# A cross-product kernel: one part of its combined weights computed row by row on TensorE instead of being moved there by DMA, and a coarser alternation of two kinds of work

## The reference

```python
# x: [512, 39, 64]   W0: [39, 39, 128]   W1: [39, 128, 128], all float32
x0 = h = x
outs = []
for W in (W0, W1):
    h = einsum('bid,bjd,ijh->bhd', x0, h, W)
    outs.append(h)
return concatenate(outs, axis=1).sum(axis=-1)      # [512, 256]
```

## Time and profile before

| what | value |
|---|---|
| median of 3 runs | 436.07 us (432.43 to 438.65) |
| profiled execution | 436.33 us, span 434.5 us |
| PE busy | 269.7 us, 62% |
| DVE, ACT, POOL busy | 160.5, 84.1, 77.5 us |
| DMA moved | 27.65 MB |
| TensorE clock, mean of the span | 0.847 |

### The profile page before, as it was taken

One profiled execution on the slowest core, in us unless ns is written; L12 is line 12 of the kernel. 1 busy time (PEld: TensorE's weight loads), 2 busy tenths in 40 slices (PEclk: granted clock), 3 DMA queues, 4 the chain that ended last, 5 costly groups with the idle time before them and its releaser, 6 DMA issues.

```text
span 434.5 us, 16676 instructions
## 1 busy us (share of the span) xinstructions
PE 269.7 (62%) x7930; PEld 235.2 (54%) x7930; DVE 160.5 (37%) x266; ACT 84.1 (19%) x105; POOL 77.5 (18%) x69
## 2 busy tenths in 40 slices
PE   5999400000000000998879797996978969789897
PEld 2448400000000000997778696895977859688796
DVE  0200001000000000996269906829369194691600
ACT  2661000000000000011113133231332313323300
POOL 2000000000000000100009910804407025070000
PEclk9999955555555555799998999998999999999999
DMA  8623475444444438001113121221212212100010
GB/s 306 277 34 38 55 124 132 42 55 51 46 51 51 47 47 178 23 5 34 34 32 82 55 74 39 70 72 32 63 51 65 54 56 63 51 8 14 7 20 8
DMA packets 25044, 27.65 MB, mean 64 GB/s; under 512 B 5712, under 2 KB 19600, under 8 KB 24720
## 3 DMA queue, kind: packets, MB, share of 16 engines
q1 hardware_dynamic: 24976, 26.59, 29.2%
HBM read 18.40 MB, written 0.52 MB: 44 GB/s over the span
## 4 chain that ended last, share of the span: by engine, by line
PE 55%; SPq 28%; issue 9%; DVE 4%; DMA 3%; ACT 0%; POOL 0%; POOLq 0%
SPq L252 28%; PE psum L458 24%; PE psum L437 15%; PE psum L396 7%; PE psum L414 6%; DMA arena<-arena 3%; PE psum L466 2%; DVE arena L345 2%; PE psum L472 1%; DMA arena<-in_w 1%; DVE arena L318 1%; DVE arena L329 0%; DVE arena L327 0%; ACT arena L360 0%; SPq L256 0%
## 5 line engine op out<-in xcount | busy, mean ns | idle before, releaser
L414 PE MATMUL psum<-arena 128*32 128x128 f32 x1690 | 54.1, 283 | 126.4 <-DVE arena L345 125.8
L220 POOL COPY arena<-arena 128x72 f32<-128x72 f32 x32 | 68.5, 2141 | 313.0 <-DMA arena<-in_x 171.6
L377 ACT COPY arena<-psum 128x920 f32<-128x920 f32 x64 | 61.1, 984 | 314.1 <-PE psum L437 314.0
L414 PEld LDWEIGHTS psum<-arena 128*32 128x32 f32 x1690 | 50.7, 113 | 130.1 <-DVE arena L345 126.3
L458 PE MATMUL psum<-arena 128*64 128x128 f32 x1840 | 111.2, 277 | 0.6 <-issue 0.6
L458 PEld LDWEIGHTS psum<-arena 128*64 128x64 f32 x1840 | 103.7, 138 | 6.1 <-issue 5.9
L437 PE MATMUL psum<-arena 64*32 64x115 f32 x4096 | 65.0, 265 | 29.5 <-issue 26.7
L437 PEld LDWEIGHTS psum<-arena 64*32 64x32 f32 x4096 | 54.9, 106 | 37.8 <-issue 37.8
L345 DVE TENSOR_TENSOR arena<-arena,psum 128x512 f32<-128x512 f32 (+1 forms) x29 | 18.4, 680 | 113.0 <-DMA arena<-arena 97.1
L318 DVE TENSOR_TENSOR arena<-arena 128x1600 f32<-128x1600 f32 x32 | 58.0, 1812 | 0.0
L336 DVE TENSOR_TENSOR arena<-psum,arena 64x256 f32<-64x256 f32 x8 | 3.3, 417 | 88.5 <-ACT arena L368 88.5
(11 more groups left out here) (13 smaller groups left out, 38.1 us busy)
## 6 DMA issues: line engine op xcount, KB each, us to landing
arena<-in_x SPq DMA_DIRECT2D x32, 312.0 KB, 3.1
arena<-arena SPq DMA_DIRECT2D x40, 57.5 KB
arena<-in_w SPq DMA_DIRECT2D x2, 768.0 KB, 7.8
arena<-in_v_first SPq DMA_DIRECT2D x1, 1520.0 KB, 11.4
arena<-in_v_second SPq DMA_DIRECT2D x1, 1520.0 KB, 14.5
arena<-in_c_x SPq DMA_DIRECT2D x2, 704.0 KB, 11.2
arena<-arena SPq DMA_DIRECT2D x24, 50.0 KB
arena<-arena SPq DMA_DIRECT2D x24, 47.5 KB
```

Source lines behind the costliest of these rows:

```text
L220: nc.gpsimd.tensor_copy(view(to, TO, (1, COPY0)), view(x + X_MAIN + 21, T, (1, COPY0)))
L377: nc.scalar.copy(view(s0[n % 2] + 8 * in_batch, (1, 2), (B, SLOTS), (2, GROUP)), bank_view(at, (BANK, 2), (GROUP, SLOTS), (1, GROUP))).the ...
L414: done = nc.tensor.matmul(bank_view(bank * BANK + j % IN_BANK * HID, (1, HID), rows=(ROWS * c, ROWS * c + ROWS)), view(v0 + row * ROWS, (1 ...
```

## The change

It has three parts. **Own weights in row form:** for each of the 128 hidden columns k and each strip c, one matmul with 32 places of W1 (read with a step of 32 words) as the stationary side and the 115 pairs as the moving side; the result has places on rows. Eight k fill two PSUM banks, and ACT copies them at once into `c0` (16 copies of 128 x 920, written with a step of 128 words). The 128 DMAs and the clearing of `c0` are gone; three DVE multiplications by a 0/1 mask clear what must not stand there. W1 is laid out in four pieces of 32 hidden columns. The loads of x, `w0_t2` and `c1_x` follow the tables directly, and DVE makes the first four units of products ahead of the masks. **Ends of batches:** `stage(n-2)` goes to the start of batch n, `take_out(n-3)` in place of `take_out(n-2)` ahead of its second unit, `store(n-2)` to its third. **Alternation:** the sums of four groups (16 pairs), then half a batch of weighing.

```diff
-        SUMS_BEHIND = {16: 0, 20: 1, 24: 2, 28: 3}
-        PRODUCTS_BEHIND = {7: 0, 10: 1, 13: 2, 16: 3}
+        SUMS_BEHIND = {10: 0, 15: 1, 20: 2, 25: 3}
...
 # gpsimd
-            nc.gpsimd.memset(view(c0, (1, ZEROED * HID)), 0.0).then_inc(c_zeroed, 1)
-                if u < PROD_RING:
-                    pool.wait_ge(c_landed, C_LANDED)
-                    pool.wait_ge(out1_ready, 2)
-                else:
+                if u >= PROD_RING:
                     pool.wait_ge(filled, 2 * (u - PROD_RING + 1))
...
 # sync
-            sp.wait_ge(c_zeroed, 1)
-            for i, (g, which, q) in enumerate(DIRECT):
-                sp.wait_ge(direct_copied, i + 1)
...
-                for f in range(4):
-                    sp.dma_start(view(c0 + j * HID, (HID, SLOTS - j), (1, HID), rows=(row + f, row + f + 1)),
-                                 view(d0[c] + (4 * g - ROW0[which] + f) * HID, (1, HID), rows=(j, SLOTS)))\
-                        .then_inc(c_landed, 16)
...
+            sp.dma_start(view(mask0, (1, len(MASKED))), mask).then_inc(mask_loaded, 16)
+            for u in range(BATCH_UNITS):
+                load_x(u)
+            (w0_t2 and c1_x, four DMAs, then load_x(4), load_x(5))
...
-                if turn == 1 and n >= 2:
+                if turn == 2 and n >= 2:
                     store(n - 2)
...
 # vector
-            dve.wait_ge(c_landed, C_LANDED)
+            products(0); products(1); (adds of out1); products(2); products(3)
+            dve.wait_ge(direct_copied, DIRECT)
+            dve.wait_ge(mask_loaded, 16)
+            for i, (j0, j1) in enumerate(MASKED):          # 15, 5 and 5 slots of 128 words
+                c = view(c0 + j0 * HID, (1, words))
+                mult(c, c, view(mask0 + i, (0, words)), ALU.mult).then_inc(c_masked, 1)
+            dve.wait_ge(c_masked, len(MASKED))
             for k in range(MIXED):
...
-                if k in PRODUCTS_BEHIND:
-                    products(PRODUCTS_BEHIND[k])
...
-                if turn == 2 and n >= 2:
-                    take_out(n - 2)
+                if turn == 1 and n >= 3:
+                    take_out(n - 3)
...
 # scalar
-                nc.scalar.copy(view(d0[2 * q + which] + (4 * g - ROW0[which]) * HID, (1, 4 * HID), rows=(0, SLOTS)),
-                               bank_view(i % DIRECT_BANKS * BANK, (1, 4 * HID), rows=(0, SLOTS)))\
-                    .then_inc(direct_copied, 1)
+                nc.scalar.copy(view(c0 + 8 * i, (4, 2), (1, 4), (HID, SLOTS)),
+                               bank_view(i % 4 * 2 * BANK, (BANK, 2), (SLOTS, 4), (1, SLOTS))).then_inc(direct_copied, 1)
...
+                if in_batch == 0 and n >= 2:
+                    stage(n - 2)
                 act.wait_ge(filled, g + 1)
...
-                if in_batch == 2 and n >= 2:
-                    stage(n - 2)
...
 # tensor
+            for i in range(DIRECT):                        # 16
+                if i >= 4:
+                    pe.wait_ge(direct_copied, i - 3)
+                for k in range(8 * i, 8 * i + 8):
+                    piece, at = divmod(k, PIECE)           # PIECE = 32
+                    if at == 0:
+                        pe.wait_ge(w1_loaded[piece], 16)
+                    for c in range(4):
...
+                        done = nc.tensor.matmul(
+                            bank_view((i % 4 * 2 + k % 8 // 4) * BANK + k % 4 * SLOTS, (1, SLOTS),
+                                      rows=(ROWS * c, ROWS * c + ROWS)),
+                            view(w1_0 + piece * PLACES * PIECE + ROW0[c % 2] * PIECE + at, (PIECE, ROWS)),
+                            view(u0 + c % 2 * LIST + c // 2 * SLOTS, (1, SLOTS)), start=True, stop=True)
+                done.then_inc(direct_filled, 1)
...
-            for u in range(BATCH_UNITS, UNITS):
-                n, turn = divmod(u, BATCH_UNITS)
-                sums(2 * u)
-                sums(2 * u + 1)
-                weigh(n - 1, turn)
-            for turn in range(BATCH_UNITS):
+            for g in range(BATCH_GROUPS, GROUPS):
+                n, in_batch = divmod(g, BATCH_GROUPS)
+                sums(g)
+                if in_batch % TURN == TURN - 1:            # TURN = 4
+                    weigh(n - 1, in_batch // TURN)
+            for turn in range(TURNS):                      # TURNS = 2
                 weigh(BATCHES - 1, turn)
```

More of the change, by code:

```diff
@@ L71, with masked_rows @@
 V_ROWS = len(v_tables())
+MASKED = [(0, 15), (15, 20), (20, COPY0 + 16)]
+def masked_rows(which, q, j):
+    if which:
+        return q == 0 or j < COPY1 + 4
+    return q == 0 and j < 20
 def cin_kernel(nc: bass.Bass, x: bass.AP, u_list: bass.AP, w1: bass.AP, v_first: bass.AP, v_second: bass.AP,
-               w0_t2: bass.AP, c1_x: bass.AP, out: bass.AP):
+               w0_t2: bass.AP, c1_x: bass.AP, mask: bass.AP, out: bass.AP):
     P, ALL_PAIRS, _ = x.shape
-    HID = w1.shape[2]
+    HID = w1.shape[1]
     HALF = P // 2
@@ L168, in cin_kernel @@
         out_stored = sem("out_stored")
[L170 to L183, removed]
         FIRST_LIST, SECOND_LIST = lists()
@@ L228, in load_x, with load_w1 @@
                              x[:, u * UNIT:(u + 1) * UNIT, :]).then_inc(x_loaded[u % X_RING], 16)
-            def load_u(which):
+            def load_w1(i):
+                words = PLACES * PIECE
+                sp.dma_start(view(w1_0 + i * words, (1, words)), w1[i]).then_inc(w1_loaded[i], 16)
+            for which in range(2):
                 sp.dma_start(view(u_raw0 + 2 * which * LIST, (1, 2 * LIST)), u_list[which]).then_inc(u_loaded[which], 16)
[L233 to L241, removed]
+            for i in range(PIECES):
                 load_w1(i)
@@ L296, in _ @@
             mult = nc.vector.tensor_tensor
-            for which in (1, 0):
+            for which in range(2):
                 raw = u_raw0 + 2 * which * LIST
@@ L304, in _ @@
             add(v, v, view(v_second0, (1, V_ROWS * ROWS)), ALU.add).then_inc(v_ready, 1)
[L305 to L308, removed]
             def products(u):
@@ L338, in take_out @@
                     view(stage0, (1, 2 * HID), rows=(0, HALF)), ALU.add).then_inc(out_ready, 1)
-            dve.wait_ge(c_landed, C_LANDED)
+            products(0)
+            products(1)
+            dve.wait_ge(out1_loaded, 64)
+            for at, second, words in ((w0_t2_0, w0_t2_second0, 4 * HID), (c1_x0, c1_x_second0, CROSS * HID)):
+                w = view(at, (1, words))
+                add(w, w, view(second, (1, words)), ALU.add).then_inc(out1_ready, 1)
+            products(2)
+            products(3)
+            dve.wait_ge(direct_copied, DIRECT)
+            dve.wait_ge(mask_loaded, 16)
+            for i, (j0, j1) in enumerate(MASKED):
+                words = (j1 - j0) * HID
+                c = view(c0 + j0 * HID, (1, words))
+                mult(c, c, view(mask0 + i, (0, words)), ALU.mult).then_inc(c_masked, 1)
+            dve.wait_ge(c_masked, len(MASKED))
             for k in range(MIXED):
@@ L385, in _ @@
         def _(pe):
-            for i, (g, which, q) in enumerate(DIRECT):
-                for piece, (f0, _) in enumerate(W1_PIECES):
-                    if 4 * g == f0 and (i == 0 or DIRECT[i - 1][0] != g):
-                        pe.wait_ge(w1_loaded[piece], 16)
[L390 to L397, removed]
-                                 view(w1_0 + 4 * g * HID, (1, 4 * HID)), start=True, stop=True).then_inc(direct_filled, 1)
+            for i in range(DIRECT):
+                if i >= 4:
[3 more added lines that the diff above has]
+                    if at == 0:
+                        pe.wait_ge(w1_loaded[piece], 16)
+                    for c in range(4):
+                        if k == 0 and c < 2:
+                            pe.wait_ge(u_ready, c + 1)
+                        done = nc.tensor.matmul(
[4 more added lines that the diff above has]
+                done.then_inc(direct_filled, 1)
             def mixed(k):
@@ L557 @@
                 v[1, :, row, r] = w0[field(c), field(l)]
-    laid_out = (("x", places[:, :, X_PLACES]), ("u_list", u_list.reshape(2, hid, -1)), ("w1", w1_places),
+    mask = _np.ones((128, len(MASKED)), f32)
+    for c in range(4):
+        for i, (j, _) in enumerate(MASKED):
+            if masked_rows(c % 2, c // 2, j):
+                at = ROWS * c + (N0 if c % 2 else N1)[0] - ROW0[c % 2]
+                mask[ROWS * c:ROWS * c + ROWS, i] = 0
+                mask[at:at + 8, i] = 1
+    w1_pieces = w1_places.reshape(hid, PLACES, 4, -1).transpose(2, 0, 1, 3)
+    laid_out = (("x", places[:, :, X_PLACES]), ("u_list", u_list.reshape(2, hid, -1)), ("w1", w1_pieces.reshape(4, hid, -1)),
                 ("v_first", v[0].reshape(hid, -1)), ("v_second", v[1].reshape(hid, -1)),
-                ("w0_t2", w0_t2.reshape(2, 128, -1)), ("c1_x", c1_x.reshape(2, 128, -1)))
+                ("w0_t2", w0_t2.reshape(2, 128, -1)), ("c1_x", c1_x.reshape(2, 128, -1)), ("mask", mask))
```

53 lines of the change are left out of this document (25 added, 28 removed).

## The result

The changed kernel takes **314.9 us** (median of 4 runs, 312.32 to 317.25) against 435.78 for the one before in the same session: ratio 0.7208, 95% interval 0.7128 to 0.7289. Its profiled execution has a span of 313.7 us. The chip has a slower state in some executions: medians here are over all runs, ratios over the fast runs alone.

The account below looks back on a forecast made before the run. SP's 128 DMAs were taken to bound the kernel until 174.3 us, then PE's work with stalls. Unit 8 at 136.6, six batches of 22.9 to 274.0, last weighing 14.4 and end 3.2: span 291.6, plus 1.8 outside, 293; range 280 to 322.

Parts of the forecast that it names:

- rival A: Sums: double bursts outrun instruction loads, PE stops 1.85 us in each of about 13 bursts, +24, 317 us; chance 0.12.
- The 128 DMAs bounded the start: Start: SP's list of 128 DMAs is the bound until 174.3 us; 121 us of the gain come from there.
- Own weights at 29.7 us and 2.0 of slow start: Own weights: 512 matmuls take 28 to 31 us, taken as 29.7, plus 2.0 for PE's slow first stretch; end at 37.8.
- rival E: Start: instruction loads crawl beside 372 GB/s of tables, so PE is not the bound: +5 us, inside the range; no separate chance.
- The start at 6.1: PE's start moves from 5.1 to some 6.1 us, as some 0.25 MB more loads ahead at 372 GB/s.
- Masks under cover: DVE's masks take 3.5 us to 44.5, covered by 6 us before PE first needs an addition at 51.9.
- Mixed stage, DVE's late unit, POOL's wait: Mixed stage ends at 102.3; DVE makes unit 4 after the last addition, 0.6 + 4.15 us; PE waits 4.5 before unit 8.
- just level with the work, so I add 0.7 for stops: Each batch: six instruction blocks take 22.3 us at 3.7 against 22.2 of work; with 0.7, 22.9 a batch, six 137.4.
- Two turns less save 0.4 us: Alternation: a turn to weighing costs 0.2 us, so two turns less save 0.4 us of a batch.
- The ends of batches get loose: New orders give DVE its lead; it needs 16.6 + 0.4 us a batch, less than PE.
- Rival C: Ends of batches: DVE still waits once per batch for an ACT copy, about 4 us x 5: 313 us; chance 0.05.
- 22 from the stalls: Of the 143 us forecast gain, 121 come from the start and 22 from the stalls.

Follow-up runs that it names:

- a4: Changed kernel with the old ends of batches and sums of two groups, then a quarter of weighing, leaving only the first part: 309.9 us, ratio 0.716.
- a6: Changed kernel, but SP issues everything behind W1 (tables, mask, x) only when the own weights have been copied: 335.6 us.
- a3: Changed kernel with `stage`, `take_out` and `store` back at their old places, half batches of weighing kept: 309.4 us, ratio 0.715.
- a1: Changed kernel with sums of two groups, then a quarter of the weighing, in place of four groups and half: 307.2 us, ratio 0.708.
- b1: Kernel before with only `stage`, `take_out` and `store` moved to their new places: 422.9 us, ratio 0.979.
- c1: Changed kernel with products of units 4 to 7 made among the additions, and sums of two groups, then a quarter of weighing: 301.8 us, ratio 0.690.
- c2: The c1 kernel with SP waiting for the first piece of W1 before it issues anything behind it: 299.1 us, ratio 0.694.
- s1: Changed kernel with 40 PE waits without work put once ahead of unit 4's sums: 315.2 us.
- t8: Changed kernel with the sums of a whole batch, then the whole weighing of the one before: 326.5 us.

## Why the prediction was right, and where its sizes were off

The forecast was 293, the range 280 to 322, the time 314.9. That is inside the range, but outside the 280 to 308 that had a chance of 0.70, and close to rival A's 317. What carried the gain was foreseen; how much the stops would take was not. By its own terms, from the spans (291.6 forecast, 313.7 measured):

| term | forecast | measured |
|---|---|---|
| start of PE | 6.1 | 8.3 |
| own weights | 31.7 | 37.0 |
| mixed stage | 64.5 | 63.7 |
| last block to unit 8 | 34.3 | 34.3 |
| six batches | 137.4 | 152.7 |
| last weighing and end | 17.6 | 17.8 |

- **The 128 DMAs bounded the start:** right. The waits of 125.4 and 97.1 us are gone, and a4, with this part alone, has 309.9, so the first part carries all of the gain that is left. It also moved the loads of x and the products of the first four units; no run parts these from the row form.
- **Own weights at 29.7 us and 2.0 of slow start:** PE's pace was right (27.3 ns a record, 28 us in all), and the slow start cost its 2.0 (0.7 in a6). The term of the sum that was off is the stops: 5.6 us where the 29.7 had room for 1.7, since I took the block pace of 3.7 us for this stage too; and the lower clock behind the longest of them cost 1.5, a term that I had at nothing. I had named slow instruction loads beside the tables as rival E, at 5 us. E is what happened, at 5.3, and a6 shows it. ACT's copies at "near 1 us" were wrong by a factor of 1.85, inside the cover of 1.9 that the text gave.
- **The start at 6.1:** PE started at 8.3. I had counted the bytes ahead of it alone (and 0.25 MB at 372 GB/s is 0.7 us, not 1.0). The start lies between 7.2 and 8.8 in the kernels with this head; what sets it is open.
- **Masks under cover:** right. They ran from 47.4 to 51, then the additions began, and PE first needed one after eight blocks, at about 58.
- **Mixed stage, DVE's late unit, POOL's wait:** within 0.8 us together. That POOL's copy waits for DVE's pause is confirmed by a3. PE's wait for it was 1.74 us where I wrote 4.5: PE got there later, as its bursts ran at part of the clock (3.3 us a unit) and stopped for 1.24. The stretch still took 34.3 us, because DVE's eight units and POOL's copy end it, not PE.
- **Batches:** PE's work was forecast at 22.2 and is 22.2 to 22.8. The step that failed is "just level with the work, so I add 0.7 for stops". A mean says little when bursts are twice as long as a block; stops took 2.6 to 3.5 a batch. This is rival A, at 1.0 to 1.8 a burst where I gave 1.85, and I gave it 0.12. The six batches took 15.3 us more than forecast; that the time still lies in the range owes to a high end drawn to take in A, and not to the sum. The evidence that I set against it, a clean stretch with the same mean demand, was from bursts of half the length.
- **"Two turns less save 0.4 us":** a turn costs 0.4, so 0.8 were saved in work, and 2 to 3 us of stops were added. a1 against the changed kernel: the third part costs 7.7 us in medians of two sessions, 0.721 against 0.708 in ratios whose intervals overlap by a hair; the profiled spans differ by 6.3 us, of which 3.9 lie in the five batches from unit 8 on.
- **The ends of batches get loose:** right in mechanism. Rival C is out: DVE's `take_out` waits for nothing in the first five batches and for ACT only at the end, and in the old kernel the move gives some 9 us (b1). But in the changed kernel it brings nothing, as half a batch of weighing hides the old stall anyway and POOL's opening is lost. So the "22 from the stalls" did not come from the mechanism that I gave: parts two and three together brought nothing (a4 309.9, changed 314.9; I don't claim that they cost 5 us, as the ratios' intervals overlap). What the stream gained came with the first part, where block borders fell elsewhere: batches of 24.8 to 25.7 us in a4, 26.5 to 28.4 before.
- **A reading:** the granted clock of the kernel before is at its lower level for eleven slices, not ten. Nothing in the sum hangs on it.

Left open: why quarter turns keep 1.0 to 1.7 us of stops a batch in a1 (0.9 to 2.0 in c1, some 1 in c2) but only 0.4 to 1.0 in b1. Where a block border falls in a burst differs between them, and s1 shows that borders can be shifted at will, but no run tried whether a better place for them removes the stops.

## What to carry to other kernels

Where PE runs many small matmuls, count instructions as a resource: stops inside a loop without a semaphore, at a constant distance in instructions, were loads of the instruction list here, and a burst must not use up more than is in store, even if the mean fits. Look for them when DMA is at its limit above all. And before taking away an engine's pause, ask who works in it: here POOL could only copy when DVE stood still.

## What the hardware did that I had not expected

- Instruction blocks came 6 us apart while data moved at 386 to 427 GB/s (PE's stops of 2.67 and 1.17 us at 23.3 and 29.5). Where stops follow each other at single borders, PE goes on 3.3 to 3.9 us after the last stop in t8, and 3.7 to 4.3 in a6's own weights.
- An ACT copy of 128 x 920 that writes with a step of 128 words takes 1.82 us, one with runs at a step of two words 0.99. Which of writing and reading order costs it was not tried.
- A wait between matmuls for a semaphore long reached is not free: with two behind each, of which one became an instruction of its own, a matmul went from 29 to 131 ns.
- POOL's copy and DVE's first operation of a unit, released by the same semaphore, end together: POOL takes 1.9 us instead of 0.25 and then gets through, in the first unit of every burst of the changed kernel and in nearly every unit of c1. Behind the mixed stage it did not get through for 25.5 us. What decides between the two was not tried.
